# A two-layer residual kernel (stencil, then prefix-softmax pooling) goes from a transposed layout with scans to natural layout with triangular products

## The chip, the core and the metric

The kernel runs on one core of one Trainium2 chip. The metric is device microseconds of one execution. Engines are named as the profile names them: PE (TensorE, matmuls; PEld is its weight load), DVE (VectorE), ACT (ScalarE), POOL (GpSimd) and SP (SyncE, which here only issues DMAs). The SP and ACT instruction streams both issue DMAs in this case. Everything is float32.

## What is computed

The input x is 2 sequences of 2048 rows with 512 channels. Two residual steps follow each other:

```
x1 = x + zX*lap_channels(x) + zY*lap_rows(x) + zR*x*(1-x)      # reflecting borders, one z per sequence
h  = tanh(x1 @ W1 + b1)            # W1: 512 x 128
s  = h @ v                         # one score a row
mask: l <= j (prompt type 0), l >= j (type 1), l != j (type 2)
pooled[j] = sum_l softmax_l(s[l] | mask)*x1[l] / count(mask[j])
out = x1 + pooled
```

With prompt type 0 for a sequence, pooled[j] is a running sum of exp(s[l])*x1[l] over l <= j, divided by the running sum of exp(s[l]) and by j+1. Both kernels have a short path for that (used when the sum of |v| is small enough for exp to be safe) and a general one for the other types.

## The kernel before

The 4096 rows are 32 tiles of 128 rows, two tiles a pair p (16 pairs), four tiles a group k (8 groups, four for each sequence, one sequence after the other). After the stencil the layout is **transposed**: 128 channels on the partitions, rows along the free axis, so that the running sums become scans on VectorE.

- SP: `load(p)` fetches 512 KB into one of four xin slots; the stores of group k-1-LAG (LAG is 4) are queued between the loads. It also fetches the border rows (`brow`), W1, b1, v and the prompt types; ACT's stream fetches zX and zR.
- ACT: `scale(p)` writes xs = zX*x (L275), `square(p)` writes loc = x*x (L281). `keep_x1T(i)` (L292) evicts the transposed x1 of a tile. `tanh(k)` (L301), `keep_scores(k)` (L307), `exp_prefix(k)` (L333), and `scale_pooled(j)` (L345), which evicts the pooled rows with their factor.
- POOL: `reflect(p)` copies the two reflecting columns of xs (L403, L404); for odd pairs from 5 on it also adds the left and the right neighbour, lr (L257). At the start it builds the identity.
- DVE: `left_right(p)` is the same addition for the other pairs (L257), `local(p)` gives loc = -zR*x*x + lr (L472). `borders(k)` adds the rows above and below a tile (L485). `prefix_rho` (L546, L548), `prefix_L` (one scan, L561), `prefix_scan` (four scans of 128x512, L572), `prefix_factor` (L585, L586), and `output(j)` (L713), which adds x1 to the pooled rows.
- PE: `stencil(i)` multiplies the tile by a tridiagonal matrix, which also transposes it, and adds the transposed loc: four times two records of L779 and one of L780. `w1_product(k)` (L790): four products of 512 columns, two records each. `scores(k)` (L796), `turn_L(k)` (L806), and the way back to rows, `back_x1(j)` (L820) and `back_Q(j)` (L835), four transposes each.

The order on every engine is written out by hand in one loop over k; each engine does its instructions strictly in that order, and each waits on semaphores counted by the others. A group's scans (k-2), its borders (k) and the outputs of group k-LAG stand in one pass of DVE's loop. The branches take the short path for both sequences here: the scans of L572 stand in that path only.

Of the kernel before, what the change touches and what calls it, by code (L numbers as in the profile page):

```python
# [5 lines left out]
NB = 2  # L30
S = 2048
D = 512
A = 128
P = 128
GB = 4
T = GB * P
NBLK = S // P
NG = S // T
TOT = NB * NBLK
GROUPS = NB * NG  # L40
DC = D // P
# [4 lines left out]
LS = 4  # L46
XP = 2
OS = 6
RS = 5
LAG = 4  # L50
WARM = 17
TAIL = GB * (GROUPS - LAG)


def build(nc, x, zX, zY, zR, itok, W1, b1, v, out):
# [4 lines left out]
    with ctx:  # L60
# [3 lines left out]
        def pb(name):  # L64
            return ctx.enter_context(nc.psum_tensor(name, [P, 512], f32))

# [3 lines left out]

        xin = sb("xin", [P, XS, 2, D])
        xs = sb("xs", [P, 2, 2, D + 2])
        lr = sb("lr", [P, 2, 2, D])
        loc = sb("loc", [P, LS, 2, D])
        x1T = sb("x1T", [P, RS, DC, T])
        G = sb("G", [P, RS, DC, T])
        hT = sb("hT", [A, T])
        srow = sb("srow", [P, S])
        outs = sb("outs", [P, OS, D])

        ident = sb("ident", [P, P])
        tri = sb("tri", [P, NB, P])
        bT = sb("bT", [P, DC, 2 * TOT])
# [3 lines left out]
        vrep = sb("vrep", [A, P])  # L87
        z = sb("z", [P, 3, NB])
        ti = sb("ti", [P, NB], i32)
        allow = sb("allow", [P, 3, NB])  # L90
# [3 lines left out]
        nzR = sb("nzR", [P, NB])  # L94
        cdia = sb("cdia", [P, NB])


        L_r = sb("L_r", [P, T + 1])
        ab = sb("ab", [P, 2, T])
        one = sb("one", [P, 1])  # L100
        spare = sb("spare", [P, 1])
        cnt = sb("cnt", [P, NBLK])
        fac = sb("fac", [P, TOT])
        vabs = sb("vabs", [A, 1])
# [4 lines left out]
        mF = sb("mF", [P, S + 1])  # L109
        mB = sb("mB", [P, S + 1])  # L110
        LF = sb("LF", [P, S + 1])
        LB = sb("LB", [P, S + 1])
        w3 = sb("w3", [P, 3, T])
        rden = sb("rden", [P, T])

        tf = rden[:, 0:NB]
        t = rden[:, 8:8 + 3 * NB].rearrange("p (k n) -> p k n", k=3)
        cnti = rden[:, 32:32 + NBLK].bitcast(i32)
        dec = sb("dec", [P, T])
        brow = dec[0:2 * TOT, :]  # L120
        wgt = sb("wgt", [P, T])
        offd = wgt[:, 0:P]
        back = L_r
        carry = sb("carry", [P, DC])

        xps = [pb(f"xps{k}") for k in range(XP)]
        xbk = [pb(f"xbk{k}") for k in range(2)]
        qbk = [pb(f"qbk{k}") for k in range(2)]
        hps = pb("hps")

        def x1_bank(j):

            return (xbk + xps)[j % 4] if j >= TAIL else xbk[j % 2]

        def q_bank(j):

            return (qbk + [hps])[(j - TAIL) % 3] if j >= TAIL else qbk[j % 2]

        lps = pb("lps")


        s_x = [sem(f"s_x_slot{k}") for k in range(XS)]
# [3 lines left out]
        s_brow = sem("s_brow")  # L146
        s_one = sem("s_one")
        s_con = sem("s_con")
        s_cnt = sem("s_cnt")
        s_pool = sem("s_pool")  # L150
        s_tri = sem("s_tri")
        s_vrep = sem("s_vrep")
        s_v1 = sem("s_v1")
        s_fast = sem("s_fast")
        s_bt = sem("s_bt")
        s_bT = sem("s_bT")
        s_xs = sem("s_xs")
        s_pad = sem("s_pad")
        s_sq = sem("s_sq")
        s_lr = [sem("s_lr_even"), sem("s_lr_odd")]  # L160
        s_loc = sem("s_loc")
        s_A = sem("s_A")
        s_xT = sem("s_xT")
        s_fix = sem("s_fix")
# [3 lines left out]
        s_srow = sem("s_srow")  # L168
        s_L = sem("s_L")
        s_Lc = sem("s_Lc")  # L170
        s_fac = sem("s_fac")
        s_G = sem("s_G")
        s_bkQ = sem("s_bkQ")
        s_bkx = sem("s_bkx")
        s_pl = sem("s_pl")
        s_o = sem("s_o")
        s_store = [sem(f"s_store{k}") for k in range(OS)]
        s_dve = sem("s_dve")
# [736 lines left out]
```

## Time and profile before

| what | value |
|---|---|
| median of 3 executions | 156.45 us (156.13 to 157.07) |
| span of the profiled execution, first to last instruction | 154.9 us |
| busy PE, DVE, ACT, POOL | 125.3, 123.2, 86.8, 34.7 us |
| mean granted clock of PE | 0.956 of full speed |
| DMA | 17.35 MB, 112 GB/s |

The page doesn't say which of the executions was profiled; its own time is known as the span alone, 154.9 us, 1.55 us under the median. In the profile, busy is the time in which an engine executes; DMA issues and waits are not in it. A matmul record's length includes its latency, and records overlap, so PE's rate is read from the chain of waits, which gives each matmul the time by which it moves the end. In a timeline row an "xN" stands for N instructions that follow each other; what stands in brackets is the engine's idle time before them and what ended it.

### The profile page before, as it was taken

To read this page: it belongs to the slowest core of one execution; us is meant where nothing else is said; L and a number is where in the kernel's file an instruction comes from. 1 tells how busy PE (TensorE), PEld (TensorE's weight loads), DVE (VectorE), ACT (ScalarE), POOL (GpSimd) and SP (SyncE) were. 2 spreads that over 40 slices of the span, in tenths; PEclk is the share of its full clock that TensorE was granted. 3 is DMA by queue.
4 is the path that set the end of the run, shared out by engine and by line. 5 is a ranking of instruction groups with operands and counts; after the bars stand their busy time and mean duration, and the time that the engine had idled before them with its cause. 6 is when DMAs were issued, how large, how long until landed. Compare 5 with 4: busy or idle time off the path is not lost.

```text
span 154.9 us, 2363 instructions
## 1 busy us (share of the span) xinstructions
PE 125.3 (81%) x792; PEld 99.9 (64%) x792; DVE 123.2 (80%) x176; ACT 86.8 (56%) x122; POOL 34.7 (22%) x50
## 2 busy tenths in 40 slices
PE   2948799969919997993599969996999999386680
PEld 2938695853819477483596659665957947284570
DVE  0087786969999989996659989999995599399991
ACT  3092969549615946955049574957513824616370
POOL 3051202404920850370004800580000000000000
PEclk9995999999996999999569999999999999999999
DMA  1791434044030404300365007400520240045396
GB/s 35 259 313 31 131 102 185 0 138 135 0 135 4 138 0 135 140 0 2 117 225 203 0 0 253 158 0 0 198 77 0 107 163 2 2 147 198 147 340 258
DMA packets 10438, 17.35 MB, mean 112 GB/s; under 512 B 1654, under 2 KB 2166, under 8 KB 10424
## 3 DMA queue, kind: packets, MB, share of 16 engines
q1 hardware_dynamic: 10136, 17.18, 32.0%
q8 instruction: 6, 0.10, 0.3%
q14 instruction: 8, 0.07, 0.2%
q10 hardware_dynamic: 288, 0.00, 0.1%
HBM read 8.79 MB, written 8.39 MB: 111 GB/s over the span
## 4 chain that ended last, share of the span: by engine, by line
DVE 47%; PE 18%; issue 16%; DMA 8%; ACT 4%; DVEq 2%; SPq 1%; POOL 0%; ACTq 0%
DVE G L572 21%; DVE lr L257 9%; DMA xin<-in_x 8%; PE xbk L820 5%; PE xps L779 4%; DVE L_r L561 4%; DVE outs L713 4%; PE qbk L835 4%; DVE loc L472 3%; PE hps L790 2%; ACT outs L345 2%; PE xps L780 2%; DVE rden L509 1%; ACT xs L275 1%; DVE fac L586 1%
## 5 line engine op out<-in xcount | busy, mean ns | idle before, releaser
L779 PE MATMUL xps<-tri,xin 128*128 128x128 f32 x256 | 48.3, 293 | 9.2 <-DVE loc L472 7.0
L779 PEld LDWEIGHTS xps<-tri,xin 128*128 128x128 f32 x256 | 41.9, 204 | 12.3 <-issue 12.2
L780 PE MATMUL xps<-ident,loc 128*128 128x128 f32 x128 | 36.3, 284 | 0.0
L292 ACT ACTIVATE x1T<-xps 128x512 f32<-128x512 f32 x32 | 19.0, 592 | 21.2 <-PE xps L780 21.2
L790 PE MATMUL hps<-x1T,W1s 128*128 128x512 f32 x64 | 29.0, 596 | 0.1
L572 DVE TENSOR_TENSOR_SCAN G<-ab,G,x1T 128x512 f32<-128x512 f32 x24 | 29.0, 1262 | 0.0
L345 ACT ACTIVATE outs<-qbk,fac 128x512 f32<-128x512 f32 x27 | 17.8, 686 | 13.2 <-PE qbk L835 9.4
L820 PE MATMUL xbk<-ident,x1T 128*128 128x128 f32 x96 | 15.6, 290 | 11.6 <-DVE outs L713 11.6
L403 POOL COPY xs<-xs 128x2 f32<-128x2 f32 x16 | 8.7, 547 | 67.9 <-ACT xs L275 67.8
L257 DVE TENSOR_TENSOR lr<-xs 128x1024 f32<-128x1024 f32 x10 | 19.0, 1900 | 5.7 <-POOL xs L404 4.2
L275 ACT ACTIVATE xs<-xin,z 128x1024 f32<-128x1024 f32 x16 | 18.3, 1143 | 7.5 <-DMA z<-in_condB_zY 4.7
L713 DVE TENSOR_TENSOR outs<-outs,xbk 128x512 f32<-128x512 f32 x24 | 15.8, 683 | 7.7 <-ACT outs L345 5.2
L820 PEld LDWEIGHTS xbk<-ident,x1T 128*128 128x128 f32 x96 | 11.6, 147 | 15.3 <-DVE outs L713 13.0
L472 DVE SCALAR_TENSOR_TENSOR loc<-loc,nzR,lr 128x1024 f32<-128x1024 f32 x16 | 20.5, 1282 | 0.4
L780 PEld LDWEIGHTS xps<-ident,loc 128*128 128x128 f32 x128 | 19.3, 151 | 0.0
L790 PEld LDWEIGHTS hps<-x1T,W1s 128*128 128x128 f32 x64 | 11.6, 191 | 11.8 <-issue 11.5
L281 ACT ACTIVATE loc<-xin 128x1024 f32<-128x1024 f32 x16 | 16.8, 1047 | 0.0
L835 PE MATMUL qbk<-ident,G 128*128 128x128 f32 x108 | 16.4, 285 | 0.0
L835 PEld LDWEIGHTS qbk<-ident,G 128*128 128x128 f32 x108 | 13.3, 147 | 2.9 <-issue 2.9
L257 POOL TENSOR_TENSOR lr<-xs 128x1024 f32<-128x1024 f32 x6 | 13.1, 2184 | 0.5
L404 POOL COPY xs<-xs 128x2 f32<-128x2 f32 x16 | 11.0, 689 | 0.0
L561 DVE TENSOR_TENSOR_SCAN L_r<-ab,L_r,one 128x512 f32<-128x512 f32 x8 | 10.3, 1286 | 0.3
(64 smaller groups left out, 101.3 us busy)
## 6 DMA issues: line engine op xcount, KB each, us to landing
xin<-in_x SPq DMA_DIRECT2D x16, 512.0 KB, 3.5
out<-outs SPq DMA_DIRECT2D x32, 256.0 KB, 2.2
W1s<-in_L_cond_W SPq DMA_DIRECT2D x1, 256.0 KB, 7.3
dec<-in_x SPq DMA_DIRECT2D x2, 62.0 KB
dec<-in_x SPq DMA_DIRECT2D x4, 2.0 KB
z<-in_condB_zX ACTq DMA_DIRECT2D x1, 1.0 KB, 4.4
z<-in_condB_zR ACTq DMA_DIRECT2D x1, 1.0 KB, 5.1
z<-in_condB_zY SPq DMA_DIRECT2D x1, 1.0 KB, 6.7
```

Source lines behind the costliest of these rows:

```text
L257: eng.tensor_tensor(lr[:, p % 2, :, :], w[:, :, 0:D], w[:, :, 2:D + 2], ALU.add).then_inc(s_lr[p % 2], 1)
L275: nc.scalar.activation(xs[:, p % 2, :, 1:D + 1], xin[:, p % XS, :, :], ACT.Copy, scale=z[:, 0, n:n + 1]).then_inc(s_xs, 1)
L292: nc.scalar.activation(x1T[:, k % RS, :, b * P:(b + 1) * P], xps[i % XP][:, :].rearrange("p (c t) -> p c t", c=DC), ACT.Copy).then_inc(s_x ...
L345: nc.scalar.activation(outs[:, j % OS, :], q_bank(j)[:, :], ACT.Copy, scale=fac[:, j:j + 1]).then_inc(s_pl, 1)
L472: vec.scalar_tensor_tensor(out=to, in0=to, scalar=nzR[:, n:n + 1], in1=lr[:, p % 2, :, :], op0=ALU.mult, op1=ALU.add).then_inc(s_loc, 1)
L572: vec.tensor_tensor_scan(G[:, k % RS, c, :], ab[:, k % 2, :], x1T[:, k % RS, c, :], start, ALU.mult, ALU.add).then_inc(s_G, 1)
L713: vec.tensor_tensor(outs[:, j % OS, :], outs[:, j % OS, :], x1_bank(j)[:, :], ALU.add).then_inc(s_o, 1)
L779: mm(to, xin[:, p % XS, i % 2, c * P:(c + 1) * P], tri[:, n, :], start=True, stop=False)
L780: last = mm(to, loc[:, p % LS, i % 2, c * P:(c + 1) * P], ident[:, :], is_transpose=True, start=False, stop=True)
L790: last = mm(hps[:, :], W1s[:, c, :], x1T[:, k % RS, c, :], start=(c == 0), stop=(c == DC - 1))
L820: last = nc.tensor.transpose(x1_bank(j)[:, c * P:(c + 1) * P], x1T[:, k % RS, c, b * P:(b + 1) * P], ident[:, :])
L835: last = nc.tensor.transpose(q_bank(j)[:, c * P:(c + 1) * P], G[:, k % RS, c, b * P:(b + 1) * P], ident[:, :])
```

## The change

The layout stays **natural**: rows on the partitions, channels along the free axis. A tile is still 128 rows but keeps 126 of them (R), so neighbouring tiles overlap by two rows and need no borders from elsewhere: 16 tiles for each sequence, and one last tile (LAST) that holds the remaining 32 rows of both. A group k is now two tiles of the first sequence and two of the second (KG = 8 groups, and LAST alone as a ninth); a pair p is two tiles of one sequence (17 pairs).

- The scans go. A tile's pooled rows are one product of a triangular matrix, weighted with exp(s), with the tile (`pooled`, 128x128 by 128x512); the sum so far comes in as row 0 of the tile, which `carry` writes: it copies the last output row of the tile before over into partition 0 of the next one.
- The denominators (`lengths`) are small products with a triangle and with ones, from a two-element running sum cs.
- The stencil is one product of 512 columns a tile, tri as the stationary operand; the local term is not added on PE. ACT computes zX*x, then x*x, then scales the square by -zR in place; POOL adds the neighbours and adds the scaled square; DVE's eviction of the stencil adds the result (`evict`).
- x1 is transposed only for the W1 product (`turn`, `keep_x1T`). Scores are products with one column.
- The z loads, W1, b1, v and the prompt types are issued by ACT's stream ahead of its first work. POOL builds masks (`masks`, 28 linked instructions) between its pairs 2 and 3; DVE's `biases` waits for them.
- The flags are computed by the same 16 linked DVE instructions. The short path is always computed; `general` follows only for a sequence that isn't short.

The core of the new code (each `eng.wait_ge(s, n)` holds that engine):

On ACT:

```diff
+            def x_scaled(p):
+                w = len(tiles_of(p))
+                for h in range(w):
+                    x_there(act, p, h)
+                if p >= 2:
+                    act.wait_ge(s_lr, p - 1)
...
+                nc.scalar.activation(xs[:, p % 2, 0:w, :], xin[:, p % XS, 0:w, :], ACT.Copy,
+                                     scale=z[:, 0, kind(p):kind(p) + 1]).then_inc(s_xs, 1)
+            def x_squared(p):
+                w = len(tiles_of(p))
+                if p >= 3:
+                    act.wait_ge(s_loc, p - 2)
+                nc.scalar.activation(sq[:, p % 3, 0:w, :], xin[:, p % XS, 0:w, :], ACT.Square).then_inc(s_xq, 1)
+                act.wait_ge(s_xq, p + 1)
...
+                nc.scalar.activation(sq[:, p % 3, 0:w, :], sq[:, p % 3, 0:w, :], ACT.Copy,
+                                     scale=nzR[:, kind(p):kind(p) + 1]).then_inc(s_sq, 1)
...
+            pair(0)
+            pair(1)
+            pair(2)
+            for k in range(KG + 1):
+                for i in group(k):
+                    keep_x1T(i)
+                pair(2 * k + 3)
+                tanh(k)
+                pair(2 * k + 4)
+                exp(k)
```

On POOL:

```diff
+            def left_right(p):
+                w = len(tiles_of(p))
+                src, to = xs[:, p % 2, 0:w, :], lr[:, p % 3, 0:w, :]
+                pool.wait_ge(s_xs, p + 1)
+                if p >= 3:
+                    pool.wait_ge(s_ev, p - 2)
+                pool.tensor_tensor(to[:, :, 0:D:D - 1], src[:, :, 1:D - 1:D - 3], src[:, :, 1:D - 1:D - 3], ALU.add)
+                pool.tensor_tensor(to[:, :, 1:D - 1], src[:, :, 0:D - 2], src[:, :, 2:D], ALU.add).then_inc(s_lr, 1)
+                pool.wait_ge(s_sq, p + 1)
+                pool.wait_ge(s_lr, p + 1)
+                pool.tensor_tensor(to, to, sq[:, p % 3, 0:w, :], ALU.add).then_inc(s_loc, 1)
...
+            left_right(0)
+            left_right(1)
+            left_right(2)
+            masks()
+            for p in range(3, PAIRS):
+                left_right(p)
```

On DVE:

```diff
+            def evict(p):
+                w = len(tiles_of(p))
+                dve.wait_ge(s_A, p + 1)
+                dve.wait_ge(s_loc, p + 1)
+                vec.tensor_tensor(X1[:, 2 * p:2 * p + w, :], xps[:, 0:w, :], lr[:, p % 3, 0:w, :], ALU.add).then_inc(s_ev, 1)
+            def biases():
+                dve.wait_ge(s_v1, 1)
+                dve.wait_ge(s_msk, 1)
...
+            def carry(j):
...
+                dve.wait_ge(s_T, to + 1)
+                dve.wait_ge(s_o, j + 1)
+                vec.tensor_copy(X1[at:at + 1, to, :], outs[0:1, j % OS, :]).then_inc(s_c, 1)
+            def weights(k):
+                i, w = GB * k, len(group(k))
+                dve.wait_ge(s_e, k + 1)
...
+                vec.tensor_tensor(M4[:, k % 2, 0:w, :], mask, each, ALU.mult).then_inc(s_M, 1)
+                if k < KG:
+                    for n in range(NB):
...
+                        vec.tensor_tensor_scan(cs[:, n, 2 * k + 1:2 * k + 3], one[:, 0:1].to_broadcast([P, 2]),
+                                               e[:, i + 2 * n:i + 2 * n + 2], cs[:, n, 2 * k:2 * k + 1],
+                                               ALU.mult, ALU.add).then_inc(s_cs, 1)
+            def output(j):
+                i = in_order(j)
...
+                vec.scalar_tensor_tensor(out=outs[:, j % OS, :], in0=U[j % 2][:, :], scalar=fac[:, i:i + 1], in1=X1[:, i, :],
+                                         op0=ALU.mult, op1=ALU.add).then_inc(s_o, 1)
+                if j < LAST:
+                    carry(j)
+            constants()
+            tridiagonal(0)
+            tridiagonal(1)
+            evict(0)
+            tridiagonal(2)
+            absolute()
+            evict(1)
+            biases()
+            for k in range(KG + 1):
+                j = GB * (k - 1)
+                if 2 * k + 2 < PAIRS:
+                    evict(2 * k + 2)
+                if k == 0:
+                    flags()
+                    first_carries()
+                else:
+                    output(j)
+                    output(j + 1)
+                if 2 * k + 3 < PAIRS:
+                    evict(2 * k + 3)
+                weights(k)
+                if k >= 1:
+                    output(j + 2)
+                    output(j + 3)
+                factors(k)
+            output(LAST)
```

On PE:

```diff
+            def stencil(p):
+                n = kind(p)
+                if p >= 1:
+                    pe.wait_ge(s_ev, p)
+                pe.wait_ge(s_tri, n + 1)
+                for h, i in enumerate(tiles_of(p)):
+                    x_there(pe, p, h)
+                    last = mm(xps[:, h, :], tri[:, n, :], xin[:, p % XS, h, :], start=True, stop=True)
+                last.then_inc(s_A, 1)
...
+            def pooled(j):
+                i, k = in_order(j), j // GB
+                pe.wait_ge(s_M, k + 1)
+                pe.wait_ge(s_c, j + 2 if j == LAST else j + 1)
+                if j >= 2:
+                    pe.wait_ge(s_o, j - 1)
+                mm(U[j % 2][:, :], M4[:, k % 2, i - GB * k, :], X1[:, i, :], start=True, stop=True).then_inc(s_U, 1)
...
+            stencil(0)
+            stencil(1)
...
+            for k in range(KG + 1):
+                j = GB * (k - 1)
+                tiles = group(k)
+                for i in tiles[0:2]:
+                    turn(i)
+                if 2 * k + 2 < PAIRS:
+                    stencil(2 * k + 2)
+                for i in tiles[2:]:
+                    turn(i)
+                if k >= 1:
+                    pooled(j)
+                    pooled(j + 1)
+                w1_product(k)
+                if 2 * k + 3 < PAIRS:
+                    stencil(2 * k + 3)
+                scores(k)
+                if k >= 1:
+                    pooled(j + 2)
+                    pooled(j + 3)
+                lengths(k)
+            pooled(LAST)
```

`scores(0)` also waits for the flags (s_fast) and the biases. `lengths(k)` waits for exp(k) and for both running sums of weights(k). SP issues load(2k+4) and load(2k+5), one DMA for each tile, and then the four stores of group k-1.

## Rows read from the trace of the kernel before

**Rows 1.** The page's first lines: span; busy us, share of the span, instructions

```profile
span 154.9 us, 2363 instructions
...
PE 125.3 (81%) x792; PEld 99.9 (64%) x792; DVE 123.2 (80%) x176; ACT 86.8 (56%) x122; POOL 34.7 (22%) x50
```

**Rows 2.** The page, chain that ended last, share of the span by engine

```profile
DVE 47%; PE 18%; issue 16%; DMA 8%; ACT 4%; DVEq 2%; SPq 1%; POOL 0%; ACTq 0%
```

**Rows 3.** Timeline, 96 to 117 us: start us, us, engine, line, operation, out<-in

```profile
96.86 1.14 ACT L275 ACTIVATE xs<-xin,z 128x1024 f32<-128x1024 f32 x1
...
97.71 4.55 DVE L572 TENSOR_TENSOR_SCAN G<-ab,x1T 128x512 f32<-128x512 f32 x4
...
97.90 1.04 ACT L281 ACTIVATE loc<-xin 128x1024 f32<-128x1024 f32 x1
...
98.83 1.18 POOL L404 COPY xs<-xs 128x2 f32<-128x2 f32 x1
...
102.32 1.89 POOL L257 TENSOR_TENSOR lr<-xs 128x1024 f32<-128x1024 f32 x1
...
102.63 2.66 DVE L257 TENSOR_TENSOR lr<-xs 128x1024 f32<-128x1024 f32 x1 [0.37 <-DVE G L572]
...
112.98 4.79 DVE L572 TENSOR_TENSOR_SCAN G<-ab,G,x1T 128x512 f32<-128x512 f32 x4
...
116.81 0.69 ACT L301 ACTIVATE hT<-hps,b1s 128x512 f32<-128x512 f32 x1 [3.28 <-PE hps L790]
```

**Rows 4.** Chain of waits in order of time: start us, us, what

```profile
93.69 0.44 PE qbk L835 x4
...
113.33 3.44 PE hps L790 x8
```

**Rows 5.** Groups of instructions by line and shape: busy us, mean ns

```profile
L292 ACT ACTIVATE x1T<-xps 128x512 f32<-128x512 f32 x32 | 19.0, 592 | 21.2 <-PE xps L780 21.2
...
L472 DVE SCALAR_TENSOR_TENSOR loc<-loc,nzR,lr 128x1024 f32<-128x1024 f32 x16 | 20.5, 1282 | 0.4
...
L713 DVE TENSOR_TENSOR outs<-outs,xbk 128x512 f32<-128x512 f32 x24 | 15.8, 683 | 7.7 <-ACT outs L345 5.2 <-issue 2.3
...
L548 DVE TENSOR_TENSOR ab<-srow 128x512 f32<-128x512 f32 x6 | 4.2, 692 | 2.3 <-ACT srow L307 2.1
...
L585 DVE TENSOR_TENSOR fac<-lps,cnt 128x4 f32<-128x4 f32 x8 | 1.3, 158 | 0.8 <-DVE G L572 0.8
```

**Rows 6.** Timeline around 27 us

```profile
27.18 1.89 POOL L257 TENSOR_TENSOR lr<-xs 128x1024 f32<-128x1024 f32 x1
...
27.25 1.85 DVE L509 TENSOR_SCALAR rden<-rden 128x2 f32<-128x2 f32 x1
```

**Rows 7.** Timeline of TensorE: first matmuls after two idle times, in brackets

```profile
46.06 0.77 PE L779 MATMUL xps<-tri,xin 128*128 128x128 f32 x2 [3.19 <-DVE loc L472]
...
135.96 0.66 PE L820 MATMUL xbk<-ident,x1T 128*128 128x128 f32 x4 [2.98 <-DVE outs L713]
```

**Rows 8.** Windows of TensorE: stretch, busy us (instructions), granted clock, DMA share, GB/s

```profile
47.00:48.00 1.00, 1.00 (x7) 0.50 0.00 0
...
136.00:137.00 1.00, 1.00 (x10) 1.00 0.30 96
```

**Rows 9.** Line 257, the addition lr: duration ns min/median/max

```profile
L257 DVE TENSOR_TENSOR lr<-xs x10: 1226/1804/2783, 9.6 to 102.6; 128x1024 f32<-128x1024 f32 x10
```

**Rows 10.** Timeline at the start and the end

```profile
1.91 0.73 POOL L418 TENSOR_SCALAR_AFFINE_SELECT wgt<-wgt 128x128 f32<-128x128 f32 x2
...
7.91 1.15 ACT L275 ACTIVATE xs<-xin,z 128x1024 f32<-128x1024 f32 x1 [4.73 <-DMA z<-in_condB_zY]
...
150.34 1.28 DVE L713 TENSOR_TENSOR outs<-outs,xps 128x512 f32<-128x512 f32 x2
```

More of the change, by code:

```diff
@@ L111, in build @@
[L111 to L142, printed above, removed]
+        srow = xin[:, 0:2, :, :].rearrange("p a b d -> p (a b d)")
+        w0 = xin[:, 2:4, :, :].rearrange("p a b d -> p (a b d)")
@@ L178, in build @@
         s_dve = sem("s_dve")
-        s_dp = [sem(f"s_dp{n}") for n in range(NB)]
         s_dg = [sem(f"s_dg{n}") for n in range(NB)]
@@ new lines, in _, with x_there @@
+            for p in range(XS):
+                load(p)
+            for k in range(KG + 1):
+                for p in (2 * k + XS, 2 * k + XS + 1):
+                    if p < PAIRS:
+                        load(p)
+                if k >= 1:
+                    for m in range(GB):
+                        store(GB * (k - 1) + m)
+            store(LAST)
+            for q in range(OS):
+                sp.wait_ge(s_store[q], stored(q))
+        def x_there(eng, p, h):
+            eng.wait_ge(s_x[p % XS][h], loaded(p, h))
@@ new lines, in exp, with pair @@
+                nc.scalar.activation(e[:, i:i + w], sps[:, i:i + w], ACT.Exp,
+                                     bias=bia[:, q:q + 1], scale=scl[:, q:q + 1]).then_inc(s_e, 1)
+            def pair(p):
+                if p < PAIRS:
+                    x_scaled(p)
+                    x_squared(p)
+            pair(0)
[8 more added lines that the diff above has]
+                exp(k)
@@ L385, in _ @@
-            for j in range(GB * (GROUPS + 1 - LAG), TOT):
-                scale_pooled(j)
         @block.gpsimd
@@ L564, in prefix_scan @@
-            def prefix_scan(k, outputs=()):
-                n, g = divmod(k, NG)
-                prefix_L(k)
-                slot_free(k)
-                dve.wait_ge(s_fix, 2 * (k + 1))
-                for c in range(DC):
-                    start = 0.0 if g == 0 else G[:, (k - 1) % RS, c, T - 1:T]
-                    vec.tensor_tensor_scan(G[:, k % RS, c, :], ab[:, k % 2, :], x1T[:, k % RS, c, :], start,
-                                           ALU.mult, ALU.add).then_inc(s_G, 1)
-                    if outputs:
-                        output(outputs[c])
-                dve.wait_ge(s_L, k + 1)
-                dve.wait_ge(s_G, DC * (k + 1))
@@ L763, in _ @@
+            dve.wait_ge(s_fast, 1)
+            short = [dve.value_load(fasti[0:1, n:n + 1]) for n in range(NB)]
+            for n in range(NB):
+                with dve.If(short[n] == 0):
+                    general(n)
+                with dve.Else():
+                    dve.nop()
         @block.tensor
@@ L823, in back_Q @@
[L823 to L836 removed]
+                for b, i in enumerate(group(k)):
+                    last = mm(sps[:, i:i + 1], hT[:, b * P:(b + 1) * P], vs[:, 0:1], start=True, stop=True)
```

889 lines of the change are left out of this document (370 added, 519 removed).

## The prediction, made before the changed kernel was run

> **What bounds the kernel now.** The page's first lines show VectorE and TensorE busy for about 80% of the span and GpSimd for 22% [rows 1]; two engines that full can't both be waiting for the same thing, so the chain of waits decides. It gives DVE 47% and PE 18% [rows 2]: VectorE's scans carry the kernel. The timeline gives the size: the four G scans of a group start at 97.71 and those of the next at 112.98 [rows 3], so a group of four tiles costs 15.3 us here. Times below are in those units, because the changed kernel also works in groups of four tiles (eight, and one tile that holds the rest).
>
> **Prices.** On TensorE the chain has one W1 product of 512 columns at 3.44 / 4 = 0.86 us and a set of four transposes at 0.44 us [rows 4]. Scores and lengths (one column each, two records a product) I take at 0.1 us a record, from the 128-column transpose, 0.11 us, as the upper bound and half of it as the lower. ACT: 1.14 us for a scaled copy of 1024 columns, 1.04 us from the start of one to the start of the next [rows 3]; 0.59 us for an eviction of 512 columns [rows 5]. POOL: 1.89 us for an addition of 1024 columns [rows 3]. DVE: 0.68 us for 512 columns from PSUM, 1.28 us for 1024 (the nearest row; it reads SBUF alone), 0.69 us for 512 from two SBUF operands, 0.16 to 0.2 us for a few elements [rows 5].
>
> **What goes and comes.** Gone from DVE: 40 scans (five a group), the additions lr and the products loc. New on DVE per group: two evictions of 1024 columns (2.5), four outputs (2.8), four carry rows (0.4 to 0.7 each, from half of 0.69 plus a start to all of it), the weights (0.69), small ones: some 9.5 us of a group. TensorE drops the transposes of loc and the way back of x1 and Q, but takes the triangular products: four stencils 3.44, sixteen transposes 1.76, W1 3.44, four pooled 3.44, scores 0.8, lengths 0.45, in all 13.3 us. By its old parts it is 16 stencil products at 0.22 and as many loc transposes at 0.11 (5.3), W1 3.44, scores 0.86, eight sets back 3.5, the L row 0.3: 13.4 us. So TensorE gains nothing, and 13.3 us is the floor of a group. ACT: two x_scaled, two squares, two scalings (6.6), four evictions 2.4, tanh 0.7, exp 0.3: 10 us. POOL: two pairs of two additions and an edge, 8.2 us. No engine is over its floor; what counts is the order.
>
> **The loop of a group**, from the end of lengths(k-1). TensorE: four transpose sets 1.76, a stencil pair 1.72, two pooled 1.72, W1 3.44: 8.64 us. ACT keeps x1T and does pair(2k+3) beside that. Then the tanh, 0.69 us long [rows 3]: with 0.2 for the end of the last product and the hand-over, and the next ACT instruction 0.1 inside it as above, 0.8. Then comes pair(2k+4), which stands on ACT's queue ahead of exp(k): 1.04 + 1.10 (the square must end before it is scaled in place) + 1.14 = 3.3, and exp 0.3: 3.6. Stencil(2k+3), scores and two pooled (4.3 us) are hidden beside it. The weights (0.69), two running sums (0.4) and hand-overs come to 1.15, the lengths to 0.45. Sum 8.64 + 0.8 + 3.6 + 1.15 + 0.45 = 14.6 us.
>
> **And the wait that is new.** POOL and DVE hinder each other in this trace. DVE's lr addition at 102.63 took 2.66 us while POOL's own, at 102.32, ran for 1.89; the small POOL copy at 98.83 took 1.18 us beside the scans, one scan's time [rows 3]. A DVE instruction on two columns, at 27.25, took 1.85 us: it ended with POOL's addition [rows 6]. So one instruction of one engine waits for one of the other, and they alternate. In the new order the second POOL addition of pair(2k+4) is released by the same scaling that exp(k) follows: it starts about 0.3 us ahead of the weights, which read two SBUF operands, and holds them for about 1.6 us. (Were the weights first, the addition would slip in between them and the running sums, and hold those.) Loop: 14.6 + 1.6 = 16.2 us. TensorE then stands idle for 16.2 - 13.3 = 2.9 us in each group; its clock was at 1.00 (2.4 GHz) after an idle time of 2.98 and at 0.50 (1.2 GHz) after one of 3.19 [rows 7, 8]. I take no fall in the loop, and keep it as the upper end.
>
> The Trainium skill bears on this (GPSIMD Engine Reference, Key points): GpSimd shares its SBUF interfaces with VectorE, and contends with DVE instructions in a 2-port mode or with two SBUF inputs. By that rule the evictions and outputs, which read PSUM and one SBUF tile, stay free, and the trace has no case of them beside a POOL addition. Were they held too, each first eviction would cost up to 1.9 us more, though most of them lie in slack.
>
> Another rule speaks against the change. The row first: the same addition takes 1.89 us on POOL [rows 3] and 1.23 us on DVE, where nothing holds it up [rows 9]. The Trainium skill (GPSIMD Engine Reference, Engine selection) says to give elementwise additions to VectorE, since GpSimd is about twice as slow with two inputs; its 4497 ns for 2048 columns would be an estimated 2250 ns for 1024. By that figure the loop would be 0.4 us longer.
>
> **The start.** z is there at 7.9 now [rows 10]; with all three on ACT's queue I take 7.2. ACT also issues W1, b1 and v before its first work; I take these as done by then. POOL has xs(0) at 8.4, and then three pairs in a row, 4.2 each (two additions of 1.89, edge, hand-overs): 12.6, and 1 for DVE instructions that come between: 22. Then the masks: 28 instructions in a chain, most small; a 128-column one takes some 0.37 with its hand-over (0.73 for two) [rows 10], the smallest perhaps 0.2: 8 us (5 to 11), so 30. DVE stands in biases() until then, and with it evict(2), stencil(3) and all that follows. Biases and eviction: 31.9. Then 16 linked flag instructions beside lr(3) and lr(4), six POOL instructions in a row until 39.2: one slips in at each boundary, and the rest takes 2.3: 41.5. Two memsets 0.6, evict(3) 1.25, weights and sums 1.1, lengths 0.45: 44.9 us. Without the alternation it is 38.5. TensorE has been idle for several microseconds by then, and by [rows 7, 8] it starts group 1 at the low clock: 2 us more.
>
> **The end.** Group 6 has half a pair: -2.3. Group 7 has no second stencil and no pair: 11.7. The last: transposes 0.44, two pooled 1.7, W1, tanh and scores 1.6, then the chain pooled, output, carry, pooled, output (0.86 + 0.2 + 0.7 + 0.5 each) up to 8.8, and 3.3 for the last store, as now (from 150.34 + 1.28 to the span's end at 154.9) [rows 1, 10]: 12.1.
>
> **Sum.** 44.9 + 2 + 6 x 16.2 - 2.3 + 11.7 + 12.1 = 165.6 us of span, against 154.9. The median is 156.45, 1.55 over the profiled span; the times don't say which execution was profiled, so I add the 1.55: 167. Some 6 to 7% slower. The loads are as many bytes, two DMAs for one: SP issues them behind the stores of the group before, 4.6 us ahead of their use, and they stay hidden; late, they would hold pair(2k+4).
>
> **Rivals.**
> - *The clock falls in every group* (0.12). The 2.9 us of idle time bring a fall, for at least some 3 us of work at half speed: +1.6 x 6 = 9.6: 177. For it: 2.9 lies close to the two cases of [rows 7]. Against it: the shorter of these brought none.
> - *POOL misses the loop, the start stays late* (0.18). The addition is done before exp, or the operands don't collide: loop 14.6, and 1.0 less is saved in group 6: 44.9 + 2 + 87.6 - 1.4 + 23.8 = 156.9, plus 1.55: 158.
> - *Faster* (0.27). The tiny flag instructions aren't queued one by one, so group 1 starts at 38.5, and the loop is 14.6: 150.5 + 1.55 = 152. If ACT's pair is hidden too, TensorE bounds at 13.4: 38.5 + 80.4 + 23.8 = 143, plus 1.55: 144. Place: lengths(k), behind ACT's exp(k). Price: 1.6 us a group and 6.4 at the start. It decides from a loop of 14.4 us with the late start, 15.4 with the early one. For it: DVE loses 40 scans of the chain [rows 2]. Against it: the alternation is there on the same kinds of instruction [rows 3, 6].
> - That the change isn't what it says: the L572 scans stand in the short path only, so both sequences take the path that the new code takes as its main one, and general() stays unused. No chance kept.
>
> **The numbers.** Forecast 0.43 (160 to 172); the three rivals 0.12, 0.18 and 0.27. About 0.5% is what a measurement of this kernel can tell from no change: 155.7 to 157.2. Faster takes the 0.27 and a little of the second rival; the same holds 0.05; slower the rest. The range reaches from 148, half into the faster case, to 175. The case of slower holds most; its own range is 158 to 177.
>
> **What would show it.** POOL busy about 80 us and DVE down to about 85; PE about 110 busy. The weights instruction, 0.69 us of work, takes 2 us or more and ends with a POOL addition; PE's largest wait is for the running sums or for exp, some 2.9 us once a group, eight times. Group starts (weights) lie 16 us apart. The first weights come at 43 us, and DVE's longest single wait, near 10 us, is for the masks. It is wrong if the weights take 0.7 us, if group 1 begins before 40, or if the groups lie under 15 us apart.

## The result, and the profile after

The changed kernel takes 183.51 us (median of 4, 183.17 to 184.05) against 156.75 us: 1.168 times as long, 95% interval 1.161 to 1.175. The forecast was slower with 0.67, at 167 us and at most 175. The direction holds, the size does not: two of the effects that it named were larger (the wait for POOL, and the fall of TensorE's clock, which it took at nothing in the loop), and one was not in it (the end). Some executions of one kernel run over 1.5% longer than its fastest, and the times below are medians of the others.

The first lines of the page after, which answer to [rows 1] and [rows 2]: span, busy times, granted clock in 40 slices (tenths), and the chain by engine.

```profile
span 182.1 us, 1738 instructions
...
PE 136.9 (75%) x476; PEld 79.3 (44%) x476; DVE 99.1 (54%) x158; ACT 80.5 (44%) x104; POOL 80.6 (44%) x89
...
PEclk9995799765799999965999799759996999999965
...
PE 48%; issue 16%; POOL 10%; ACT 10%; DVE 8%; DMA 3%; SPq 1%; ACTq 0%; POOLq 0%; DVEq 0%
```

DVE is down from 123.2 to 99.1 us busy, and POOL up from 34.7 to 80.6. The forecast had 85, 80 and, for PE, 110 (now 136.9): DVE's busy time contains its instructions' waits for POOL, and PE's the stretches at the low clock. The chain has moved from DVE (47%) to PE (48%), but the products at full clock don't bound it: the row of clocks has 14 places below 9, and TensorE stands idle in most groups, as shown next. The mean granted clock is 0.866, against 0.956 before.

The timeline of one group of the changed kernel, 94 to 99 us. Columns as in [rows 3]; L278 is the scaling of pair(2k+4), L305 exp(k), L366 POOL's second addition, L511 the weights, L516 the running sums, L742 the first product of lengths(k).

```profile
94.40 1.15 ACT L278 ACTIVATE sq<-sq,nzR 128x1024 f32<-128x1024 f32 x1
...
95.45 0.34 ACT L305 ACTIVATE e<-sps,bia,scl 128x4 f32<-128x4 f32 x1
95.68 2.34 POOL L366 TENSOR_TENSOR lr<-lr,sq 128x1024 f32<-128x1024 f32 x1
95.82 2.74 DVE L511 TENSOR_TENSOR M<-maskT,e 128x512 f32<-128x512 f32 x1 [1.19 <-ACT e L305]
98.49 0.34 DVE L516 TENSOR_TENSOR_SCAN cs<-one,cs,e 128x2 f32<-128x2 f32 x2
...
98.97 0.36 PE L742 MATMUL sps<-e,triC 128*128 128x4 f32 x2 [2.99 <-DVE cs L516]
```

This is the forecast's new wait. POOL's addition starts 0.14 us ahead of the weights, which need 0.69 us of work and take 2.74, until 0.54 us after the addition's end. TensorE stands idle for 2.99 us, as in the forecast (2.9). What the forecast did not take is in the windows of TensorE (stretch, busy us, granted clock, DMA share, GB/s). The first row lies behind the idle time of 2.99 us that ends at 62.76, the other three behind the one that ends at 98.97:

```profile
64.00:65.00 1.00, 1.00 (x6) 1.00 0.74 238
...
99.00:100.00 1.00, 1.00 (x6) 0.63 0.00 0
...
101.00:102.00 1.00, 1.00 (x4) 0.50 0.62 197
...
103.00:104.00 1.00, 1.00 (x6) 1.00 0.92 307
```

Behind the first the clock stays at 1.00; behind the second it falls to 0.50 just as the work resumes. The starts of the weights show what it does to the groups:

```profile
43.32 0.69 DVE L511 TENSOR_TENSOR M<-maskT,e 128x512 f32<-128x512 f32 x1 [0.27 <-ACT e L305]
...
59.60 2.74 DVE L511 TENSOR_TENSOR M<-maskT,e 128x512 f32<-128x512 f32 x1 [1.19 <-ACT e L305]
...
76.18 2.74 DVE L511 TENSOR_TENSOR M<-maskT,e 128x512 f32<-128x512 f32 x1 [1.19 <-ACT e L305]
...
95.82 2.74 DVE L511 TENSOR_TENSOR M<-maskT,e 128x512 f32<-128x512 f32 x1 [1.19 <-ACT e L305]
...
114.06 2.74 DVE L511 TENSOR_TENSOR M<-maskT,e 128x512 f32<-128x512 f32 x1 [1.19 <-ACT e L305]
...
133.54 2.74 DVE L511 TENSOR_TENSOR M<-maskT,e 128x512 f32<-128x512 f32 x1 [1.19 <-ACT e L305]
...
150.53 1.63 DVE L511 TENSOR_TENSOR M<-maskT,e 128x512 f32<-128x512 f32 x1
```

From one start to the next it is 16.3, 16.6, 19.6, 18.2, 19.5 and 17.0 us. The idle time behind each 2.74 us of weights is the same 2.99 us, five times, but the clock fell around the end of four of them, for 1.6 to 3.1 us of lost time each, and not at the first (59.60 to 76.18, 16.6 us). From here on 16.6 us is the group without a fall.

The start and the end, in rows: DVE's wait for the masks (L465), two of the flags (L471, L473) beside POOL's additions, PE's wait for the last flag, and the first lengths; then the last output.

```profile
29.93 0.34 DVE L465 TENSOR_SCALAR bia<-scl,sps 128x1 f32<-128x1 f32 x2 [9.51 <-POOLq L409]
...
32.32 2.25 DVE L471 TENSOR_SCALAR t<-tf 128x2 f32<-128x2 f32 x1
...
34.80 1.76 DVE L473 TENSOR_SCALAR t<-t 128x2 f32<-128x2 f32 x1
...
41.06 1.84 PE L727 MATMUL sps<-vs,hT 128*128 128x1 f32 x8 [6.17 <-DVE fasti L484]
...
44.43 0.56 PE L742 MATMUL sps<-e,triC 128*128 128x4 f32 x2 [1.53 <-DVE cs L516]
```

```profile
174.16 0.75 DVE outs L538
```

Group 1 begins at 45.3 us (forecast 44.9). The last output ends at 174.9, 7.2 us before the end of the span; the forecast had 3.3.

### The profile page after: what moved, and what is told of

The parts are those of the page before. It is cut to its first block, busy times and chain, and to the rows that moved or that the text cites. A ratio compares the mean times of both kernels' runs of the same rounds, so it can differ in the third digit from the quotient of the medians.

```text
span 182.1 us, 1738 instructions
## 1 busy us (share of the span) xinstructions
PE 136.9 (75%) x476; PEld 79.3 (44%) x476; DVE 99.1 (54%) x158; ACT 80.5 (44%) x104; POOL 80.6 (44%) x89
## 3 DMA queue, kind: packets, MB, share of 16 engines
q1 hardware_dynamic: 9276, 16.92, 28.8%
## 4 chain that ended last, share of the span: by engine, by line
PE 48%; issue 16%; POOL 10%; ACT 10%; DVE 8%; DMA 3%; SPq 1%; ACTq 0%; POOLq 0%; DVEq 0%
PE hps L716 14%; PE U L751 10%; PE tps L705 10%; PE xps L697 9%; ACT xs L267 4%; POOL lr L366 4%; DMA xin<-in_x 3%; POOL lr L363 3%; ACT sq L274 3%; PE sps L742 2%; PE sps L727 2%; PE sps L743 2%; DVE allow L475 1%; DVE cs L516 1%; ACT e L305 1%
## 5 line engine op out<-in xcount | busy, mean ns | idle before, releaser
L697 PE MATMUL xps<-xin,tri 128*128 128x512 f32 x66 | 39.8, 734 | 7.9 <-DVE X L454 7.6
L454 DVE TENSOR_TENSOR X<-xps,lr 128x1024 f32<-128x1024 f32 (+1 forms) x17 | 20.2, 1188 | 36.9 <-PE xps L697 32.6
L366 POOL TENSOR_TENSOR lr<-lr,sq 128x1024 f32<-128x1024 f32 (+1 forms) x17 | 38.8, 2283 | 2.4
L751 PE MATMUL U<-X,M 128*128 128x512 f32 x66 | 32.2, 606 | 1.2 <-issue 1.2
L363 POOL TENSOR_TENSOR lr<-xs 128x1020 f32<-128x1020 f32 (+1 forms) x17 | 31.2, 1836 | 0.0
L716 PE MATMUL hps<-x1T,W1s 128*128 128x512 f32 (+1 forms) x72 | 29.9, 558 | 0.7 <-ACT x1T L287 0.7
L538 DVE SCALAR_TENSOR_TENSOR outs<-U,fac,X 128x512 f32<-128x512 f32 x33 | 24.4, 739 | 5.4 <-PE U L751 5.3
L705 PEld LDWEIGHTS tps<-ident,X 128*128 128x128 f32 x132 | 20.7, 184 | 5.4 <-issue 5.4
L511 DVE TENSOR_TENSOR M<-maskT,e 128x512 f32<-128x512 f32 (+1 forms) x9 | 17.0, 1891 | 10.8 <-ACT e L305 10.8
L705 PE MATMUL tps<-ident,X 128*128 128x128 f32 x132 | 22.7, 329 | 0.0
L500 DVE COPY X<-outs 1x512 f32<-1x512 f32 x32 | 19.3, 603 | 3.3
L716 PEld LDWEIGHTS hps<-x1T,W1s 128*128 128x128 f32 x72 | 13.1, 190 | 16.3 <-issue 15.3
L278 ACT ACTIVATE sq<-sq,nzR 128x1024 f32<-128x1024 f32 (+1 forms) x17 | 19.1, 1123 | 0.6
L742 PE MATMUL sps<-e,triC 128*128 128x4 f32 x16 | 3.5, 288 | 17.1 <-DVE cs L516 17.1
```

Source lines behind the costliest of these rows:

```text
L363: pool.tensor_tensor(to[:, :, 1:D - 1], src[:, :, 0:D - 2], src[:, :, 2:D], ALU.add).then_inc(s_lr, 1)
L366: pool.tensor_tensor(to, to, sq[:, p % 3, 0:w, :], ALU.add).then_inc(s_loc, 1)
L454: vec.tensor_tensor(X1[:, 2 * p:2 * p + w, :], xps[:, 0:w, :], lr[:, p % 3, 0:w, :], ALU.add).then_inc(s_ev, 1)
L500: vec.tensor_copy(X1[at:at + 1, to, :], outs[0:1, j % OS, :]).then_inc(s_c, 1)
L538: vec.scalar_tensor_tensor(out=outs[:, j % OS, :], in0=U[j % 2][:, :], scalar=fac[:, i:i + 1], in1=X1[:, i, :], op0=ALU.mult, op1=ALU.add) ...
L697: last = mm(xps[:, h, :], tri[:, n, :], xin[:, p % XS, h, :], start=True, stop=True)
```

## The experiments

Twelve kernels, each the changed kernel with one edit unless said otherwise. Experiments 1 to 4, 7, 8 and 11 rest on two executions each, number 10 on one. Times of the kernel before beside them were 156.4 to 156.8 us.

### 1. The weights ahead of POOL's addition

```diff
                 pool.wait_ge(s_lr, p + 1)
+                if p >= 4 and p % 2 == 0:
+                    pool.wait_ge(s_cs, p - 2)
                 pool.tensor_tensor(to, to, sq[:, p % 3, 0:w, :], ALU.add).then_inc(s_loc, 1)
```

> Edit: from pair 4 on, POOL's second addition of an even pair waits until the running sums of weights(k) are done, so that the weights never wait for it; nothing is left out. Theory A (port wait plus low clock): the weights instruction falls from 2.74 to about 0.69 us, TensorE's idle time before lengths from 2.99 to about 0.9 us, the granted clock stays at 1.00 after it, and the group shrinks from 16.6 to 19.6 us to about 14.6. From weights(0) at 43.3 to weights(6) the trace of the changed kernel has 107.2 us; six groups of 14.6 less the half pair make 86: about 162 to 164 us in all. Rival B (the wait on the port is slack, the chain is elsewhere): the time moves by less than 2 us, since the addition moved later makes evict(2k+4) late instead. Rival C (the low clock has another cause than the idle time): the weights shrink, but the clock still falls, and the time is about 172.

Measured: 161.22 us, 22.3 less. The timeline of this kernel (L513 the weights, L744 the lengths):

```profile
86.24 0.69 DVE L513 TENSOR_TENSOR M<-maskT,e 128x512 f32<-128x512 f32 x1 [1.19 <-ACT e L305]
...
87.34 0.36 PE L744 MATMUL sps<-e,triC 128*128 128x4 f32 x2 [0.94 <-DVE cs L518]
...
100.76 0.69 DVE L513 TENSOR_TENSOR M<-maskT,e 128x512 f32<-128x512 f32 x1 [1.19 <-ACT e L305]
```

The weights take 0.69 us, TensorE idles 0.94 us, its clock stays at 1.00 in the loop, and from the second weights to the sixth a group is 14.52 us long. Theory A holds, and its 14.6 is the forecast's own sum without the port wait. Here the wait and the low clock go together, so the next run takes the clock alone.

### 2. Filler on TensorE, the wait stays

```diff
                     pooled(j + 3)
+                if k < KG - 1:
+                    for _ in range(8):
+                        mm(hps[:, 0:P], ident[:, :], ident[:, :], start=True, stop=True)
                 lengths(k)
```

> Edit: eight extra products of 128 columns (about 1.8 us) on TensorE just ahead of lengths(k), k up to 6, into a bank that nobody reads; TensorE's idle time of 2.99 us is cut to about 1.2 us and the wait of the weights stays. Theory A: the clock no longer falls in the groups after 79, 98, 117 and 136 us, whose length goes from 18.2 to 19.6 back to 16.6 us: 7.6 us less over groups 2 to 5, about 176 us. The weights stay at 2.74 us. Rival C (idle time is not what lowers the clock): no change, 183.5. Rival D (the fall is hidden by the chain over ACT): no change in time, though the clock stays at 1.00.

Measured: 175.62 us, 7.9 less.

```profile
77.18 2.75 DVE L511 TENSOR_TENSOR M<-maskT,e 128x512 f32<-128x512 f32 x1 [1.19 <-ACT e L305]
...
80.34 0.35 PE L742 MATMUL sps<-e,triC 128*128 128x4 f32 x2 [1.22 <-DVE cs L516]
...
93.76 2.75 DVE L511 TENSOR_TENSOR M<-maskT,e 128x512 f32<-128x512 f32 x1 [1.19 <-ACT e L305]
```

The wait of the weights is as before, the idle time is 1.22 us, the clock no longer falls, and groups 2 to 5 are 16.58 us each. More work on TensorE made the kernel faster. From the second weights to the seventh it takes 81.7 us, against 150.53 - 59.60 = 90.9 in the changed kernel: the falls cost 9.3 us. The filler's own work takes back 1.2 of it in group 1, where it runs at the low clock of the start (60.60 - 43.16 against 59.60 - 43.32), and 0.9 in group 7. Experiment 1 then adds up: 9.3 for the falls, 5 x 2.05 + 0.9 = 11.2 for the wait of the weights, and 2.4 for sums of group 0 that come earlier (41.51 against 43.93) make 22.9, and 22.3 were measured (23.2 between the two profiled spans).

### 3 and 4. The start: masks first, or flags first

Masks first puts `masks()` ahead of `left_right(0)` on POOL. Flags first:

```diff
             evict(1)
+            dve.wait_ge(s_v1, 1)
+            flags()
             biases()
...
                 if k == 0:
-                    flags()
                     first_carries()
```

> Edit: POOL builds the masks ahead of pair 0 instead of between pairs 2 and 3, in time in which it now waits for the first xs (2.8 to 9.4 us). Theory A: pair 0 begins at about 9.7 as now, DVE no longer waits 9.5 us in biases, lr(3) starts at 25.4 instead of 30.0; the flags still alternate with POOL's additions. Group 1 begins at about 36 to 38 instead of 45.3: 174 to 176 us. Rival E (the start is bounded by the W1 product and the tanh, the masks are slack): under 2 us less.

> Edit: DVE computes the 16 flags ahead of biases, in the time in which it waits for the masks, and not beside POOL's additions of pairs 3 and 4. Theory A (they alternate with POOL's additions one by one): the flags take 3.3 us instead of 9.6, and group 1 begins at about 40 instead of 45.3: 178 us. Rival F (the flags' 9.6 us are slack, since evict(3) has to wait for POOL's addition of pair 3 anyway, which ends at 34.5): the weights of group 0 come at the same time, or are held by an addition of pair 4 instead, and under 2 us are won.

Measured: 180.46 us (3.0 less) for masks first, and 178.55 us (5.0 less) for flags first, whose other execution, the profiled one, took 181.60. In both profiles group 1 begins at 40.0 instead of 45.3. For the masks theory A was 2 to 4 us too hopeful on the start and 4 to 6 on the time: the flags ran into POOL's additions of pairs 3 and 4, and four of them took 1.8 to 2.3 us. For the flags it was right on the start, but by the way that rival F describes. There the flags still took 5.9 us, since one ran into an addition of pair 2, and the weights met an addition of pair 4. The rows of flags first, at its start:

```profile
34.21 1.23 DVE L454 TENSOR_TENSOR X<-xps,lr 128x1024 f32<-128x1024 f32 x1 [2.17 <-POOL lr L366]
34.21 1.89 POOL L363 TENSOR_TENSOR lr<-xs 128x1020 f32<-128x1020 f32 x1
...
35.54 1.11 DVE L511 TENSOR_TENSOR M<-maskT,e 128x512 f32<-128x512 f32 x1
36.24 2.60 POOL L366 TENSOR_TENSOR lr<-lr,sq 128x1024 f32<-128x1024 f32 x1
36.57 2.42 DVE L516 TENSOR_TENSOR_SCAN cs<-one,cs,e 128x2 f32<-128x2 f32 x2
```

The weights (35.54) got in between two additions, and the two running sums behind them, 0.35 us of work, then took 2.42 us beside the addition. That is the case which the prediction put in brackets: whoever comes first, the addition is paid for within the chain. The first two rows show the opposite: an eviction (L454, from PSUM and one SBUF tile) ran its usual 1.23 us while POOL's addition ran too. By the rule of the Trainium skill quoted in the prediction (GPSIMD Engine Reference, Key points) that is so, and the trace agrees.

Two rows of experiment 6, below, show that a small instruction on SBUF isn't always held either (L530 is a reciprocal of four elements, with one operand):

```profile
32.94 1.89 POOL L363 TENSOR_TENSOR lr<-xs 128x1020 f32<-128x1020 f32 x1
...
33.81 0.18 DVE L530 RECIPROCAL fac<-lc 128x4 f32<-128x4 f32 x1
```

The spans of the two profiles are 179.8 and 179.9 us, 2.3 and 2.2 under the changed kernel's, where the start alone won 5.3. Experiment 11 asks where the rest is.

### 5. exp ahead of the pair

```diff
                 tanh(k)
-                pair(2 * k + 4)
                 exp(k)
+                pair(2 * k + 4)
```

> Edit: ACT does exp(k) ahead of pair(2k+4) instead of behind it; nothing else moves. Theory A: both the 3.3 us of the pair and the addition that it releases leave the loop, so that TensorE is the bound: 8.64 us, then stencil 1.72, scores 0.9, two pooled 1.72, lengths 0.45, some 13.4 to 13.8 us a group instead of 14.5 (weights-first run) or 16.6 to 19.6 (changed kernel), with the clock at 1.00. The start gains too, since pair 4's addition no longer stands beside the flags: group 1 at about 41. In all about 154 us. Rival B (ACT is short of time: the pair, moved behind the scores, makes x1T late and the W1 product waits for it): a group of 15 us or more, 163 us or more.

Measured: 154.7 us, 0.988 of the kernel before (0.984 to 0.992). One line moved wins 28.8 us. Groups from the second on are 13.46 us, TensorE's own work.

### 6. All three

> Edit: the masks ahead of pair 0, the flags ahead of the biases, and exp(k) ahead of pair(2k+4), together. Theory A: group 1 begins at about 34 to 35, groups of 13.4 to 13.8 us, end as in the changed kernel (11.8 + 17.1 us from the lengths of group 6): about 146 us, faster than both kernels. Rival: the three share their gain as masks-first and flags-first may (each began group 1 at 40.0 and gave part back in later groups): about 152.

Measured: 144.7 us (two executions; two more took 147.0 and 148.8), 11.9 us or 7.6% under the kernel before on the same chip (156.6); no interval is given for it. The loop in its timeline (L728 the scores, L743 the first product of the lengths, L752 pooled, L706 the next group's transposes):

```profile
71.53 1.96 PE L752 MATMUL U<-X,M 128*128 128x512 f32 x4
71.71 0.35 ACT L305 ACTIVATE e<-sps,bia,scl 128x4 f32<-128x4 f32 x1 [1.81 <-PE sps L728]
71.96 1.14 ACT L267 ACTIVATE xs<-xin,z 128x1024 f32<-128x1024 f32 x1
...
72.09 0.69 DVE L511 TENSOR_TENSOR M<-maskT,e 128x512 f32<-128x512 f32 x1
...
73.33 0.28 PE L743 MATMUL sps<-e,triC 128*128 128x4 f32 x2
...
73.69 1.07 PE L706 MATMUL tps<-ident,X 128*128 128x128 f32 x8
```

exp comes straight behind the scores and the pair behind exp; POOL starts its additions only when the weights are done, and the lengths follow the pooled products with no idle time before them. Group 1 begins at 33.4 us (lengths end, forecast of this run 34 to 35).

### 7. Without the branch over the general path

Left out are the general path and the branches at the end of ACT's and DVE's programs.

> Left out: the general path for prompt types 1 and 2, with the branches over it at the end of ACT's and DVE's programs; for these inputs it does not run. In the changed kernel 7.2 us lie between DVE's last output (174.91) and the end of the span, 3.3 us in the kernel before; SP waits 3.9 us of them at the last barrier. Theory G: those 3.9 us are the engines jumping over the long general code after their last output; without it the tail is 3.3 us, about 179.5 us in all. Rival H (the last store, of 32 rows on few partitions, lands late): the tail stays at 7 us, 183.5.

Measured: 179.18 us, 4.3 less. SP's own waits, first in the changed kernel, then in this one (L35 is the barrier at the end):

```profile
SPq L35 <- PEq L35: 3.9, 1, 3.9
```

```profile
SPq L35 <- PEq L35: 0.2, 1, 0.2
```

The wait at the end goes from 3.9 to 0.2 us, and the tail behind DVE's last output is 177.1 - 174.3 = 2.8 us. Theory G holds, and rival H falls: some 4 us of the changed kernel are the engines getting past code that doesn't run. The run left out the flag reads and branches together with the code behind them, so it doesn't show which of these takes the time.

### 8. The local term back on DVE

```diff
-                act.wait_ge(s_xq, p + 1)
...
-                nc.scalar.activation(sq[:, p % 3, 0:w, :], sq[:, p % 3, 0:w, :], ACT.Copy,
-                                     scale=nzR[:, kind(p):kind(p) + 1]).then_inc(s_sq, 1)
...
-                pool.tensor_tensor(to, to, sq[:, p % 3, 0:w, :], ALU.add).then_inc(s_loc, 1)
...
+                vec.scalar_tensor_tensor(out=lr[:, p % 3, 0:w, :], in0=sq[:, p % 3, 0:w, :], scalar=nzR[:, q:q + 1],
+                                         in1=lr[:, p % 3, 0:w, :], op0=ALU.mult, op1=ALU.add).then_inc(s_loc, 1)
                 dve.wait_ge(s_A, p + 1)
```

> Edit: one part of the change undone. ACT squares only, POOL adds the neighbours only, and DVE joins the two in one instruction of 1024 columns (1.28 us) ahead of each eviction, as the kernel before does; layout, products and order stay. Theory A: pair(2k+4) is 1.15 us shorter, and no second POOL addition stands before the weights, though the first one still may, for 0.9 us: a group of about 14.3 us, clock at 1.00; the masks begin after three single additions, so group 1 starts at about 35: about 152 us. Rival B (DVE has no room for 2.6 us more a group and becomes the bound, or its additions now wait for POOL's): a group of over 15.5 us, 160 us or more.

Measured: 153.43 us, 0.980 of the kernel before (0.975 to 0.984), 30.1 less than the changed kernel.

```profile
92.44 1.89 POOL L358 TENSOR_TENSOR lr<-xs 128x1020 f32<-128x1020 f32 x1
...
93.43 1.44 DVE L510 TENSOR_TENSOR M<-maskT,e 128x512 f32<-128x512 f32 x1
```

The weights are held only by the first addition, and take 1.44 us; a group is 14.09 us (forecast 14.3). With the local term back on DVE, and nothing else undone, the natural layout with its products beats the kernel before by 2%: the placing of that term costs 30.1 us in this order of ACT's work. 8.6 us of it lie ahead of the first weights (34.72 against 43.32), the rest in the loop, where ACT's scaling, POOL's second addition and the low clock all go at once.

### 9. The three moves and the local term on DVE

> Edit: the run with the three moves (masks first, flags first, exp first; 145.9 us) and the local term joined on DVE as in the run local-on-DVE. Theory A: the loop is TensorE's 13.46 us already, so nothing changes there; DVE takes 2.6 us more work a group but its carry copies no longer wait for a second addition; only the start gains, group 1 at about 32 instead of 33.6: about 144 us. Rival B (DVE, 103.6 us busy of 143 with waits in it, becomes the bound): a group of over 14 us, 150 us or more.

Measured: 145.74 us, 0.925 of the kernel before (0.917 to 0.933). Groups are 13.34 us, but the first is 15.0, at the low clock; group 1 begins at 33.3, not 32. So it is no better than experiment 6 (144.7), though POOL and ACT have less to do: TensorE is the bound in both, and the low clock in the first group makes the difference of 1 us.

### 10. The second addition not in place

POOL writes to a tile of its own, and the eviction reads that.

> Edit: POOL's second addition writes to a tile of its own instead of in place, and the eviction reads that one. The prediction priced it at 1.89 us, and it took 2.34. Theory I (writing over an operand costs the 0.45 us): 1.89 us, weights 2.29 us instead of 2.74, groups shorter by 0.45. Theory J (it is the second tile as an operand, where the neighbours' addition reads one tile twice): still 2.34 us and the same time, but for what the clock does.

Measured, in one execution: 183.87 us. The groups of POOL's additions in this kernel (mean ns of one):

```profile
L367 POOL TENSOR_TENSOR ab<-lr,sq 128x1024 f32<-128x1024 f32 x16 | 37.8, 2360 | 2.3
L364 POOL TENSOR_TENSOR lr<-xs 128x1020 f32<-128x1020 f32 x16 | 30.2, 1886 | 0.0
```

Still 2.36 us. Theory I falls. J's mechanism (two different tiles as operands) fits. The size is not the reason: in the kernel before, an addition of 1024 columns from one tile took 1.89 us [rows 3]. But the two additions also differ in their offsets, and no run varied those: which of the two makes it 2.35 and not 1.89 stays open.

### 11. Filler and masks first

> Edit: the filler products (175.6 us alone) and the masks first (180.5 us alone) together. Masks-first began group 1 5.3 us earlier and won only 3. Theory A (the rest was given back because TensorE's clock fell in more of the groups, which the filler prevents): all of the 5.3 us are kept, 170 us, groups of 16.58 us throughout. Rival K (the late groups wait for something else that has not moved, loads or stores): 172.5 us or more.

Measured: 170.69 us, 4.9 less than filler alone, with groups 2 to 5 at 16.58 us. Theory A holds: what masks-first won at the start was given back by the clock. In masks first the clock fell behind all five idle times of 2.99 us (from one lengths to the next 18.2, 19.6, 18.2, 19.5, 15.9 us), in the changed kernel behind four (16.6, 19.6, 18.2, 19.5, 15.9). That is 1.7 us; another 1.5 went in its first group, which began at 40.0 with the clock low until 45.6, where the changed kernel's began at 45.3 with the clock low until 48.0.

### 12. The three moves and filler at the start

Eighteen extra products between stencil 0 and stencil 1, on top of experiment 6.

> Edit: the run with the three moves (145.9 us, 144.7 to 148.8), and 18 extra products of 128 columns (about 4 us) on TensorE between stencil 0 and stencil 1, where it stands idle for 4.7 us now and runs stencil 1 at the low clock (3.78 us instead of 1.88). Theory A (the low clock of stencil 1 is on the path of the start): stencil 1 takes 1.9 us, group 1 begins 1 to 2 us earlier, at about 32, and the time is about 144 us with less spread. Rival L (POOL's three pairs bound the start): stencil 1 is faster, and the time stays at 145 to 146 us.

Measured: 149.1 us, 0.956 of the kernel before (0.949 to 0.963): slower than experiment 6 by 4.4 us, which neither theory expected. Its start (L479, L482 flags, L363 and L366 POOL's additions of pair 3):

```profile
15.99 1.98 PE L698 MATMUL xps<-xin,tri 128*128 128x512 f32 x4 [0.70 <-DVE X L454]
...
25.30 1.89 POOL L363 TENSOR_TENSOR lr<-xs 128x1020 f32<-128x1020 f32 x1
25.31 1.90 DVE L479 SCALAR_TENSOR_TENSOR cbase<-t,cbase 128x2 f32<-128x2 f32 x1
...
27.33 2.34 POOL L366 TENSOR_TENSOR lr<-lr,sq 128x1024 f32<-128x1024 f32 x1
27.45 2.25 DVE L482 TENSOR_SCALAR fast<-fast,sps 128x2 f32<-128x2 f32 x1
...
31.54 1.98 PE L698 MATMUL xps<-xin,tri 128*128 128x512 f32 x4 [3.75 <-DVE X L454]
```

and the same stretch in experiment 6:

```profile
25.19 0.16 DVE L479 SCALAR_TENSOR_TENSOR cbase<-t,cbase 128x2 f32<-128x2 f32 x1
...
28.61 1.88 PE L698 MATMUL xps<-xin,tri 128*128 128x512 f32 x4
```

Stencil 1 does take 1.98 us instead of 3.78. But everything behind it comes 1 us earlier, POOL's pair 3 too (25.30), while DVE's flags do not; the last ones now meet the two additions, the eviction behind them is 3.9 us late, and stencil 3 starts at 31.54 instead of 28.61. The lengths of group 0 begin at 35.84 instead of 33.00, 2.8 us later, and group 1, the 5 us from 35 on at a clock of 0.66 where experiment 6 has 1.00, lasts 14.97 instead of 13.27. These two are 4.5 us, and account for the 4.4.

## Why the prediction was right in direction and wrong in size

The forecast's sum, against the trace of the changed kernel, each part from the end of one set of lengths to the next:

| part | forecast | trace |
|---|---|---|
| start, to the lengths of group 0 | 44.9 | 45.3 |
| groups 1 to 6, with the low clock of the first | 2 + 97.2 - 2.3 = 96.9 | 107.9 |
| group 7 | 11.7 | 11.8 |
| last tile and end | 12.1 | 17.1 |
| span | 165.6 | 182.1 |

- **TensorE's floor of 13.3 us a group**: right. Experiments 5 and 6, with nothing else in the chain, give 13.46.
- **The loop of 14.6 us without the port wait**: right; 14.52 in experiment 1. That ACT's order (pair ahead of exp) is what opens it to ACT and POOL is shown by experiment 5.
- **The port wait**: right in kind and place; experiment 1 removes it. Its size was wrong, since POOL's second addition was priced at the neighbours' 1.89 us [rows 3] and takes 2.34; the 2250 ns that the prediction worked out beside its sum, and didn't use, were nearer. The weights lose 2.05 us and not 1.6, the group without a fall is 16.6 and not 16.2: 2.3 us of the difference. The full wait came five times and not eight: the weights of group 6 take 1.63 us, those of groups 0 and 7 0.69.
- **"I take no fall in the loop"**: this is the step that failed. It put at nothing what its first rival, held at 0.12, priced at 9.6 us, and the range, up to 175, left out that rival's 177. Experiment 2 prices the falls at 9.3 us. The step rested on two cases, idle times of 2.98 and 3.19 us [rows 7, 8], and read a bound out of them that isn't there: of five equal idle times of 2.99 us four came with a fall and one with none, and in experiment 12 the clock stayed at 1.00 through an idle time of 3.75 us and behind it. With the falls and the addition (9.3 + 2.3) the loop's missing 11.0 us are accounted for within 1 us. What decides whether the clock falls at a given idle time stays open.
- **The end**: 3.3 us were carried over from the kernel before, "as now". The changed kernel has its general path in one piece behind the last output; experiment 7 shows some 4 us for passing it. The forecast had looked at that code only to say that it isn't run. The other 1.1 us of the end lie in the last tile's chain of products, outputs and carries, whose parts, as the prediction writes them, come to 8.3 and not to its 8.8.
- **The start**: right to 0.4 us, by its two reasons. The flags took 9.6 us beside POOL's additions, for 3.3 us of work. The masks took 6.8 us (22.96 to 29.78), not 8, and DVE waited 9.5 for them.
- **The rival "faster"** (0.27): both of its conditions can be had, by moving lines; with them the kernel is at 144.7 us, where that rival had 144 to 152. Nothing in the change itself brought them about.
- **The eviction beside an addition**: not held, 1.23 us beside an addition of 1.89 us (experiment 4, the first two rows); no cost.

## What to carry to other kernels

An in-order engine's queue is part of every loop that passes through it: look for the one long instruction that stands ahead of a short one on which another engine waits, since moving that line was worth 28.8 us here. Work taken from VectorE to GpSimd is not taken off VectorE's path when the two hold each other up: price each GpSimd addition as a possible wait of its full length for a VectorE instruction with two operands in SBUF, or a copy, a cast or a tensor-scalar instruction on SBUF, even one of two elements, and ask what releases the two at the same moment. And an idle time of about 3 us on TensorE should be priced with the low clock behind it, in the upper end of a range at the least.

## What the runs showed of the hardware that was not expected

- The same idle time of TensorE, 2.99 us, is followed by a clock of 0.50 or of 1.00 from one group to the next of one run. In the loop 1.2 us of idle time (experiments 2 and 11) and 0.94 (experiment 1) never were followed by a fall. The last idle time alone doesn't decide: at the start, the clock stayed at 1.00 behind 3.75 us (experiment 12) and 1.72 (experiment 6), and fell within 2 us behind 1.53 (experiments 9 and 12).
- An addition of 1020 or 1024 columns takes 1.89 us on POOL with both operands from one tile, and 2.34 to 2.36 us for 1024 with two tiles, in place or not (experiment 10).
- A copy of one row of 512 columns within SBUF takes 0.41 us on DVE alone and up to 2.05 us beside an addition on POOL; an eviction from PSUM of 1024 columns takes 1.23 us either way, and a reciprocal of four elements in SBUF 0.18 us beside one (experiment 6).
- At the end of this program some 4 us go on getting past a long path that is not taken, with its flag reads and branches (experiment 7).
- Making TensorE faster at the start made the kernel slower by 4.4 us (experiment 12), since it moved POOL's additions onto DVE's flags.
